# Cross-attention kernel: bias sums in sixteen rows of one bank, other orders in the setup, in slots 0 to 3 and around the folds of N, and two-batch tiles in slot 10

## The reference, cut to what matters

```python
def _L0_xattn_ref(x, latents, shift, scale, ...):    # x: layernormed context, latents: x
    xn = layernorm(x, ln1_w, ln1_b)                   # context, 16 batches x 64 rows x 512
    ln = layernorm(latents, ln2_w, ln2_b)             # 16 batches x 1024 rows x 512
    q = ln @ Wq                                       # 16 heads x 64
    k, v = split(xn @ Wkv, 2)
    q = q * (1.0 + scale[:, None, :, None]) + shift[:, None, :, None]
    attn = softmax(einsum('bihd,bjhd->bhij', q, k) * DIM_HEAD ** -0.5)
    return einsum('bhij,bjhd->bihd', attn, v) @ Wout
x = x + _L0_xattn_ref(ctx_1024, _layernorm(x), fside, fside, ...)
x = x + tanh(((_layernorm(x) @ weight) @ aux_weight1) @ aux_weight2 + ffn_bias)
```

## Time and profile before

| what | value |
|---|---|
| median of 3 runs | 2051.66 us (2050.03 to 2053.55) |
| the profiled execution's own time | 2051.34 us |
| its span in the trace | 2049.5 us |
| PE busy | 2027.4 us (99%) |
| DVE, POOL, ACT busy | 1520.5, 1349.7, 1319.4 us |
| granted TensorE clock, mean | 0.999 |
| DMA | q1 holds nearly all: 429.54 MB, 74.6% of 16 engines' span |

### The profile page before, as it was taken

The page is one execution under the profiler, slowest core; times in us unless marked ns, Lnnn a source line. Parts: engine busy times, 40 slices in busy tenths (PEclk is TensorE's granted clock), DMA queues, the critical chain, the costliest instruction groups (busy, mean ns, idle before and its releaser), DMA issues.

```text
span 2049.5 us, 31380 instructions
## 1 busy us (share of the span) xinstructions
PE 2027.4 (99%) x9180; PEld 1681.4 (82%) x9180; DVE 1520.5 (74%) x2414; ACT 1319.4 (64%) x3005; POOL 1349.7 (66%) x1466
## 2 busy tenths in 40 slices
PE   9999999999999999999999999999999999999998
PEld 7777878888888888888888888888888888888887
DVE  7567777776777777777777777777777777787776
ACT  4455667666766666666666667666666666666654
POOL 3136766766676776767676776767677676767564
PEclk9999999999999999999999999999999999999999
DMA  7657988878787887878788787878767576666653
GB/s 263 197 176 211 271 232 245 251 225 248 222 227 206 219 223 208 226 204 231 195 232 219 208 224 206 230 197 217 211 185 211 174 207 179 200 184 191 178 170 118
DMA packets 502490, 431.54 MB, mean 211 GB/s; under 512 B 54832, under 2 KB 408240, under 8 KB 502320
## 3 DMA queue, kind: packets, MB, share of 16 engines
q1 hardware_dynamic: 502320, 429.54, 74.6%
HBM read 251.33 MB, written 178.06 MB: 210 GB/s over the span
## 4 chain that ended last, share of the span: by engine, by line
PE 86%; DVE 3%; DMA 2%; ACT 2%; issue 2%; POOL 2%; SPq 2%; DVEq 0%; ACTq 0%; POOLq 0%
PE bank L161 34%; PE bank L1176 21%; PE bank L166 17%; PE bank L1179 10%; DMA m_scratch<-evac 1%; PE bank L880 1%; PE bank L879 1%; POOL area L1458 1%; POOL area L1465 1%; DVE N_lo L987 0%; DVE area L1319 0%; SPq L321 0%; DVE row_max L1324 0%; DVE turned L1341 0%; ACT bank L992 0%
## 5 line engine op out<-in xcount | busy, mean ns | idle before, releaser
L1458 POOL TENSOR_TENSOR area<-area,row_max 128x256 f32<-128x256 f32 x512 | 353.8, 712 | 145.8 <-DVE row_max L1324 145.8
L1176 PE MATMUL bank<-N_hi,pT_hi 128*128 128x512 f32 x1024 | 398.7, 389 | 2.6 <-DVE N_lo L987 1.3
L161 PE MATMUL bank<-M_hi,xT_hi 128*128 128x512 f32 x1024 | 398.7, 389 | 0.0
L161 PE MATMUL bank<-M_lo,xT_hi 128*128 128x512 f32 x1024 | 398.7, 389 | 0.0
L1176 PE MATMUL bank<-N_lo,pT_hi 128*128 128x512 f32 x1024 | 398.6, 389 | 0.0
L1227 ACT CAST pT_hi<-turned 128x512 fp32r<-128x512 f32 x256 | 159.1, 622 | 337.4 <-DVE turned L1341 337.4
L1465 POOL TENSOR_TENSOR area<-area,row_inv 128x512 f32<-128x512 f32 x256 | 269.2, 1052 | 114.7 <-DVE row_inv L1333 114.6
L1482 POOL TENSOR_TENSOR area<-area 128x512 f32<-128x512 f32 x127 | 165.4, 1303 | 239.3 <-ACT area L1266 239.3
L1330 DVE TENSOR_REDUCE row_sum<-area 128x8 f32<-128x512 f32 x256 | 174.4, 681 | 167.5 <-ACT area L1222 166.7
L1350 DVE TENSOR_TENSOR pT_lo<-turned,pT_hi 128x512 fp32r<-128x512 f32 x256 | 196.1, 766 | 119.2 <-ACT pT_hi L1227 119.2
L166 PE MATMUL bank<-M_hi,xT_lo 128*128 128x512 f32 x1024 | 273.9, 389 | 0.8 <-POOL xT_lo L1025 0.7
(11 more groups left out here) (183 smaller groups left out, 3923.3 us busy)
## 6 DMA issues: line engine op xcount, KB each, us to landing
p_scratch<-area SPq DMA_DIRECT2D x256, 256.0 KB, 2.6
p_moved<-p_scratch SPq DMA_DIRECT2D x512, 128.0 KB, 4.3
area<-x_dram SPq DMA_DIRECT2D x128, 256.0 KB, 4.5
area<-x_turned_dram SPq DMA_DIRECT2D x128, 256.0 KB, 4.0
x_scratch<-area SPq DMA_DIRECT2D x127, 256.0 KB, 3.0
x_moved<-x_scratch SPq DMA_DIRECT2D x508, 64.0 KB, 3.5
y_dram<-area SPq DMA_DIRECT2D x127, 256.0 KB, 3.6
land<-m_scratch SPq DMA_DIRECT2D x120, 256.0 KB, 2.8
```

Source lines behind the costliest of these rows:

```text
L161: mm = eng.matmul(ps, sh, mv, start=(n == 0), stop=False)
L1176: pe.matmul(O_ps[:], st(pT_hi, k), n_cols(mv, k), start=(k == 0 and mv is N_hi), stop=False)
L1458: last = pool.tensor_tensor(s, s, row.to_broadcast([P, 2, 4, J2]), ALU.subtract)
```

## The change

- **Bias sums.** The ones become one column a head in the block `bdv`; with a shifted window of it (`to_row`) the stationary operand has its ones in one row position a head, so that the eight pairs of a half, two matmuls each, accumulate in sixteen rows of one bank, one bank a half. PE no longer waits for an evacuation between them; ACT evacuates twice 16 rows instead of 16 times 128. The stores are still 32 DMAs: sixteen of half 0 beside kv 28 to 31, sixteen of half 1 in slots 0 to 3, four a slot, after place C's store. The load of x tile 6, in slot 4, waits for all of them, since it takes their buffer.
- **Setup orders.** Separate lists for SP, ACT, DVE and POOL after the front. PE does turn 3 before w3_lo 3 and turns 4 to 7 one kv later; ACT does turns 4 to 7 after the evacuations of kv 3, 5, 6 and 7; DVE goes on with its context tiles without standing between kv steps; POOL takes the low parts of chunks 11 and 13 too. The load of context tile 7 stands after kv 3 and behind a chunk load that waits for chunk 10's split.
- **M1 stores.** m1_raw takes its pieces in another order; slot 0 waits for the first four stores only. Slot 0 waits for the bias evacuations 1 and 2 (before: 15 and 16).
- **Slots 0 to 3.** xT_hi of tile 0 is made by POOL instead of ACT; POOL subtracts the maximum of half 0 before xT_lo of tile 1 in slot 0, and makes xT_lo(t+1) before it normalises in slots 2 and 3.
- **Folds of N.** ACT and DVE do folds 0 and 1 first, then the P work, with ACT's folds 2 to 7 after pT_hi, and DVE's fold 2 between `turn_p` and pT_lo, folds 3 to 7 after.
- **Tiles.** Tiles 28 to 31 stand in slot 10 instead of 9, all later ones a slot later. Tile 28 waits for the low part of fold 6; slot 9's fold 2 waits for the sum of tile 26 (`s_tsum` 27).

```diff
 pe_steps: ("w3_hi", 3), ("w3_lo", 3), ("turn", 3)  ->  ("w3_hi", 3), ("turn", 3), ("w3_lo", 3)
+        W3_LO = (2, 3, 0, 1)
-            some("turn", 2, 3) + some("split", 7, 8) + some("w3", 0, 1, 2, 3) + [("stats", 4), ("norm", 4)]
+            some("turn", 2, 3) + some("split", 7, 8) + some("w3", *W3_LO[:2]) + [("stats", 4), ("norm", 4)] + some("w3", *W3_LO[2:]) + \
+            [("stats", 5), ("norm", 5), ("turn", 4), ("split", 10), ("stats", 6), ("norm", 6), ("turn", 5), ("stats", 7), ("norm", 7)] + \
+            some("turn", 6) + some("split", 12) + some("turn", 7)
+        beside_sp = {2: some("split", 10), 3: some("load", 7), 4: some("split", 11), 6: some("split", 12), 8: some("split", 13),
+                     24: [("k0_load", 0)], 27: [("x0", 0)]}
+        beside_act = {0: some("split", 10), 1: some("split", 11), 3: some("turn", 4), 4: some("split", 12), 5: some("turn", 5),
+                      6: some("turn", 6), 7: some("turn", 7) + some("split", 13), 26: [("k0", 0)], 27: [("k0", 1)]}
-            pe_steps += [("kv", n)] + ([("turn", {1: 4, 3: 5, 4: 6, 5: 7}[n])] if n in (1, 3, 4, 5) else [])
+            pe_steps += [("kv", n)] + ([("turn", {2: 4, 4: 5, 5: 6, 6: 7}[n])] if n in (2, 4, 5, 6) else [])
-        POOL_LO = (6, 9)
+        POOL_LO = (6, 9, 11, 13)
...
         def load_x(sp, u, r):
             at_least(sp, s_xout[r], 16 * (u // RING))
+            if u == 6:
+                sp.wait_ge(s_kbst[1], 16 * H)
+        def store_bias(sp, half, four):
+            q, h = four // 2, four % 2
+            if four == 0:
+                sp.wait_ge(s_kbo, half + 1)
+            rows = bias_scratch[half * 8:half * 8 + 8].rearrange("b (q h s k j) -> q h k b s j", q=2, h=2, s=2, k=4)[q, h]
+            own = bias_out[half][four * 4:four * 4 + 4, :].rearrange("k (b s j) -> k b s j", b=8, s=2)
+            for k in range(4):
+                sp.dma_start(rows[k:k + 1], own[k:k + 1]).then_inc(s_kbst[half], 16)
...
-                tile_at[2 + m, place] = 4 * m + i
+                tile_at[2 + m + m // (TPB - 1), place] = 4 * m + i
...
             store("C")
+            if t < 4:
+                store_bias(sp, 1, t)
...
                     if t == TPB + 1 and p == 2:
-                        pe.wait_ge(s_tsum, 31)
+                        pe.wait_ge(s_tsum, 27)
... slot_act
+            folds = m == 1 and 1 < t < T
+            if folds:
+                fold_n_act(act, t - 1, range(2))
             if tile_of(t - 1):
                 pT_hi_part(0, t - 1)
             if m == 0 and 0 < t < T:
                 v_prepare_act(act, t // TPB)
-            if m == 1 and 1 < t < T:
-                fold_n_act(act, t - 1, range(8))
+            if folds:
+                fold_n_act(act, t - 1, range(2, 8))
... slot_dve
+            if folds:
+                fold_n_dve(dve, t - 1, range(2))
...              turn_p(0, t - 1)
+                if folds:
+                    fold_n_dve(dve, t - 1, range(2, 3))
                 pT_lo_part(0, t - 1)
-            if m == 1 and 1 < t < T:
-                fold_n_dve(dve, t - 1, range(8))
+            if folds:
+                fold_n_dve(dve, t - 1, range(3, 8))
... slot_pool
+            if t in (2, 3):
+                xT_split_lo(pool, t + 1)
             if t < T:
                 normalise(0)
                 normalise(1)
```

More of the change, by code:

```diff
@@ L173, in build @@
         RING_W = 5
-        m1_raw = [stage_more[:, i * BANK:(i + 1) * BANK] for i in range(4)] + xr[2:4] + [S[0][:, i * BANK:(i + 1) * BANK] for i in range(2)]
+        M1_EARLY = 4
+        m1_raw = [S[0][:, i * BANK:(i + 1) * BANK] for i in range(2)] + xr[2:4] + [stage_more[:, i * BANK:(i + 1) * BANK] for i in range(4)]
         stage = stage + [stage_more[:, i * 2 * D:(i + 1) * 2 * D] for i in range(2)]
@@ L211, in build @@
[L211 to L216, removed]
@@ new lines, in build @@
+        beside_dve = {27: [("k0", 0)], 28: [("k0", 1)]}
+        for g in range(4):
+            beside_dve[(9, 10, 12, 14)[g]] = some("fold", g)
+            beside_act[11 + 2 * g] = some("split", WQ_FIRST + g)
+            beside_dve[11 + 2 * g] = some("split", WQ_FIRST + g)
+            beside_sp[11 + 2 * g] = some("split", WQ_FIRST + g)
+            beside_act[(20, 22, 25, 28)[g]] = some("split", WQ_FIRST + 4 + g)
+            beside_dve[(21, 23, 26, 29)[g]] = some("split", WQ_FIRST + 4 + g)
@@ L226, in build @@
             pe_steps += [("kb", n - 19)] if 19 <= n < 31 else []
-            later_steps += [("kv", n)] + beside.get(n, [])
+            sp_later += [("kv", n)] + beside_sp.get(n, [])
+            act_later += [("kv", n)] + beside_act.get(n, [])
+            dve_later += [("kv", n)] + beside_dve.get(n, [])
+        pool_later = [("kv", n) for n in range(4 * PAIRS)]
         kv_where = lambda n: (1 - n // 16, (n // 8) % 2, n % 8)
@@ L251, in build @@
         s_ku, s_kuh, s_kul, s_kb, s_kbo = (sem(n) for n in ("s_ku", "s_kuh", "s_kul", "s_kb", "s_kbo"))
-        s_kbst = [sem(f"s_kbst{i}") for i in range(3)]
+        s_kbst = [sem(f"s_kbst{i}") for i in range(2)]
         s_kvst = [sem(f"s_kvst{i}") for i in range(2)]
@@ L279, in load_ctx @@
                 sp.dma_start(ctx_in[i % 3], ctx_t[i]).then_inc(s_ctx[i % 3], 16)
[L281 to L287, removed]
             for c in range(5):
@@ L362, in setup_pool @@
             pool.wait_ge(s_const, 3)
-            for step, i in pool_front + later_steps:
+            for step, i in pool_front + pool_later:
                 if step == "stats":
@@ L392, in setup_act @@
         def setup_act(act):
-            for step, i in act_front + later_steps:
+            for step, i in act_front + act_later:
                 if step == "split":
@@ L442, in setup_dve @@
             for half in range(2):
-                own = slice(half * DH, (half + 1) * DH)
-                dve.memset(bdv[own, own].bitcast(F32), 1.0).then_inc(s_ones, 1)
-            for step, i in dve_front + later_steps:
+                dve.memset(bdv[half * DH:(half + 1) * DH, ONE_AT[half]:ONE_AT[half] + 1].bitcast(F32), 1.0).then_inc(s_ones, 1)
+            for step, i in dve_front + dve_later:
                 if step == "stats":
@@ L532, in bias_sums @@
             pe.wait_ge(s_kul, k + 1)
-            at_least(pe, s_kbo, k - 1)
-            pe.matmul(kb_ps[k % 2][:], head_ones, ku_hi[k % 2][:], start=True, stop=False)
-            pe.matmul(kb_ps[k % 2][:], head_ones, ku_lo[k % 2][:], start=False, stop=True).then_inc(s_kb, 1)
+            half, p = k // PAIRS, k % PAIRS
+            row = p // 4 * 8 + p % 4
+            to_row = bdv[:, ONE_AT[0] - row:ONE_AT[0] - row + P]
+            pe.matmul(kb_ps[half][:], to_row, ku_hi[k % 2][:], start=(p == 0), stop=False)
+            pe.matmul(kb_ps[half][:], to_row, ku_lo[k % 2][:], start=False, stop=(p == PAIRS - 1)).then_inc(s_kb, 1)
         def setup_pe(pe):
@@ L682, in load_bias @@
             if b < 2:
-                for i, w in enumerate(s_kbst):
-                    sp.wait_ge(w, 32 * len(range(i, PAIRS if b == 0 else 2 * PAIRS, 3)))
+                sp.wait_ge(s_kbst[b], 16 * H)
             sp.dma_start(bias, bias_scratch[bass.ds(b, 1), :].to_broadcast([P, INNER])).then_inc(s_bin, 16)
```

97 lines of the change are left out of this document (48 added, 49 removed).

## The result

The changed kernel takes 2082.65 us (median of 5 runs, 2080.05 to 2082.72), the kernel before 2051.66 us (median of 5 runs as well): a ratio of 1.0149, with a 95% interval of 1.0135 to 1.0162. It is slower by 31.0 us; 25.8 were forecast. 2082.65 lies in the range of 2066 to 2083, near its upper end and 0.65 us above the 2073 to 2082 given for the main case.

What follows compares the result with a forecast made beforehand. PE, busy 99% of the span, was taken to bound the kernel. From 2051.34 us the terms 25.85 - 2.2 - 2.65 + 1.3 - 1.4 + 4.9 gave +25.8, 2077.1 us, with a range from 2066 to 2083.

Steps and rivals of the forecast that it cites:

- main case: Whole kernel: all terms of the sum as forecast, about 2077 us (2073 to 2082), chance 0.45.
- Folds: Fold slots: folds 6 and 7 wait for low parts of N, 2.0 us a slot; thirteen slots +26.0, slot 25 +1.15.
- cascade: Fold slots: low parts 4 and 5 later than the next scores, or folded P late at O; 2091 us, chance 0.08.
- Slot 9: Fold slot 9: three earlier waits, 3.3 us with restarts, of which 2.0 come back; -1.3 us.
- Bias sums and the fold of M: Setup: kb's waits for ACT's evacuation go, -2.2 us; PE's wait for banks at the fold of M goes, -2.65.
- Setup orders: Setup: a turn's 1.5 us wait goes, but context tile 7 lands later and kv 8 begins at 61.2, not 59.89; +1.3 us.
- Slots 0 to 3: Slots 0 to 3: first O waits some 0.5 us less, tile 4's wait for xT_lo goes (0.9); -1.4 us.
- SP's queue: Slots 3 to 6: half 1's bias stores delay k_raw loads; PE stalls about 1.0, 3.4 and 0.5 us; +4.9 us.
- What was there to win: PE's waits: few and single, nearly all in the setup and slots 0 to 9; about 10 us in 2050.
- hidden lag: Rival, slots 4 to 6: fold cost as forecast, but SP's lag costs 0; 2072.2 us, chance 0.30.
- faster case: Rival, fold slots: fold 6 isn't late and folds cost 0; 2042 us, 2047 with SP's lag; chance 0.07.
- cheaper folds: Rival, fold slots: 1.5 us a slot; 2066 us with SP's lag hidden, 2070.5 with it; chance 0.08.

Runs made afterwards that it cites:

- Experiment 1: The changed kernel with ACT's and DVE's order in the fold slots as in the kernel before; 2056.51 us, 1.0032.
- 2: The kernel before with only the new order of ACT and DVE in the fold slots; 2078.65 us, 1.0142.
- Experiment 3: The changed kernel with ACT's cast of fold 2 moved ahead of pT_hi, DVE as changed; 2066.36 us, 1.0082.
- 11: Experiment 9 with DVE's folds 0 to 4 ahead of the turn and ACT's folds 0 to 5 ahead of pT_hi; 2043.58 us, 0.9965.
- 12: The changed kernel with DVE's folds 0 to 4 ahead of the turn and ACT's folds 0 to 5 ahead of pT_hi; 2053.09 us, 1.001.
- experiment 5: Experiment 4 with the low parts of chunks 11 and 13 made by DVE instead of POOL; 2052.69 us, 1.0009.
- experiment 4: Experiment 1 with half 1's bias stores moved out of slots 2 and 3 into slots 0 and 1; 2049.58 us, 1.0001.
- experiment 9: Experiment 6 with two DMAs instead of four for four bias rows, half 1's all in slot 0 ahead of P's store; 2046.94 us, 0.9985.
- 6: Experiment 4 with the setup orders of the kernel before, but the sixteen-row bias sums; 2052.34 us, 1.0011.
- Experiment 7: Experiment 6 with the loads of x and of x transposed of slots 2 to 7 issued by ACT instead of SP; 2054.5 us, 1.0021.

## Why the prediction was right, and where not

- **Folds.** Right in mechanism, place and size: 27.5 us in 14 slots, 27.15 forecast. Fold 6 at 5.45, fold 7 at 6.65, 2.0 a slot; measured 5.46, 6.67 and 2.01. Experiments 1 and 2 show it from both sides. Experiment 3 shows that half of it is ACT's place ahead of fold 2; the other half, DVE's ahead of fold 3, is read from the timelines and wasn't moved by itself, but 11 and 12, which move both, lose nothing. No cascade came.
- **Slot 9.** Forecast -1.3, measured +0.5 with slot 10. The waits of tile C and of the tile's sum went, as said. What the sum lacked is the clock: behind the 1.46 and 0.23 us waits of slot 9 comes a stretch at the lower level that costs 1.7 us (below).
- **Bias sums and the fold of M.** Right: between 80 and 160 us PE loses 0.2 us instead of 5.4, a gain of 5.2, 4.85 forecast.
- **Setup orders.** Mis-sized: +1.3 forecast, +3.7 measured up to 80 us (from the same ledger, 12.3 against 8.6, of which 0.9 falls in the first 25 us). The wait at kv 8 is there, 1.9 us (2 forecast), but kv 8 starts at 63.49 instead of 61.2, since turn 7 stands at 58.23 instead of 56.0. Turns 6 and 7 wait 2.15 and 1.5 us. Turn 6's wait comes from a DVE instruction stretched beside POOL's new low part, and experiment 5 shows that it only hides turn 7's. The working began tile 7's norm at the landing, put at 52.9; it landed at 53.89, and DVE began at 55.07. In its order stands the low part of turn 5 ahead of it. That waited for ACT, and ACT, one step earlier in its order, for the store of an earlier product to free its buffer, a wait that the working had at nothing. ACT, then DVE:

```profile
53.35 0.59 ACT L431 COPY area<-bank 128x512 f32<-128x512 f32 x1 [3.76 <-DMA kv_scratch<-area]
```

```profile
54.46 0.69 DVE L484 TENSOR_TENSOR N_lo<-bank,N_hi 128x512 fp32r<-128x512 f32 x1 [1.26 <-ACT N_hi L427]
55.07 0.69 DVE L451 BATCH_NORM_STATS2 area<-area 128x6 f32<-128x512 f32 x1
```

- **Slots 0 to 3.** Half right: tile 4's wait for xT_lo went (0.9 of the 1.4), but the first O waits as long as before (1.4 against 1.3 us), so the 0.5 didn't come.
- **SP's queue.** Slots 0 to 8 lose 4.5 more, 3.5 forecast with the -1.4. The forecast lag is there: the second load of k_raw in slot 3 issues at 194.71 instead of 192.89, 1.8 later. But that is less than the 2.1 to spare, so the lag alone gives no stall in slot 4, and the 1.0 forecast doesn't follow from the numbers beside it. The stall, 1.8 us, came because PE, without its waits further ahead, was at tile A 2.6 us sooner (197.3 without the stall, against 199.90), while the low part of k_parts was ready 1.2 later (199.04 against 197.83). 1.6 us more go to the lower clock behind it. Slot 5's 3.4 didn't come. In slot 6 1.3 us came instead of 0.5, but experiment 4 shows that most of it is no lag of the bias stores. So the sum of this term came near by luck, its parts were not right. What the prediction took from the Trainium skill, DMA: Bandwidth & Descriptors, section "Issuing engines are not separate DMA queues", that the stores would cost next to nothing wherever they stand, doesn't hold in this kernel: moving eight of them took slot 4's wait away, and merging them was worth 5.4 us in experiment 9 against 6.
- **What was there to win.** The prediction's list of PE's waits leaves out four (1.5, 1.5, 1.3 and 0.5 us): they come to 16 us, not some 11. No term of its sum rests on that.
- **Rivals.** The hidden lag is out by slot 4's wait, the faster case and the cheaper folds by the 1.22 and 0.24 us waits of every fold slot.
- **Still open.** Experiment 1 lies 6.6 us above before instead of 2 to 3. Its trace has tile A's waits of 2.4 us and two stretches at the lower clock in the setup, 1.5 us each, but experiment 4's trace has such stretches too. Three of its six executions, at 2057.8 to 2058.0 us, have a mean granted clock of 0.997, the other three, at 2053.9 to 2055.3, 0.998 to 1.000; what they did differently no trace shows. Why experiment 7 lost is open too. Since one execution's first 25 us differ by 1 to 2 us from the next one's, differences below that between single traces aren't read as effects.

## What to carry to other kernels

Where two engines follow a third through a ring of buffers, count for each instruction put between them what the ring has in hand: four banks gave 0.5 us here, and the P work put in around fold 2 cost 2.0 us a slot, the same work put in after fold 4 (DVE) and fold 5 (ACT) nothing. Before moving something to save a wait, look whether the engine that would start sooner waits for the bottleneck anyway, as ACT and DVE did at folds 0 and 1. And a gain in the setup shows only if the queue that carries the next stage's transfers gains too; look at it for transfers that one DMA could do instead of four.

## What the runs showed of the hardware

- **The clock behind a wait.** Behind the 1.80 us wait of PE in slot 4, eight matmuls of 512 columns are 0.43 us apart instead of 0.23, 1.6 us lost; granted clock by window (PE, PEld, DVE, ACT, POOL busy, then PEclk), 0.59 there, which is the level of 1.2 GHz for most of it, and 1.00 again from 204 us:

```profile
199.20:203.40 4.20, 4.20 (x13) 3.33 (x14) 4.13 (x8) 3.06 (x9) 1.43 (x2) 0.59 0.73 219
204.00:208.00 4.00, 4.00 (x21) 3.35 (x20) 2.49 (x7) 3.43 (x10) 2.94 (x4) 1.00 0.85 252
292.00:295.60 3.60, 3.60 (x10) 2.79 (x11) 3.23 (x6) 1.37 (x4) 0.73 (x1) 0.53 0.00 1
```

It doesn't follow every such wait: the kernel before shows none behind its 2.49 us wait, nor the changed one behind 2.15 us at 53.35, while experiment 1 has one behind the same wait, with the same setup orders.
- **DVE beside POOL.** The DVE instruction that started at 50.44 ended at 53.21, 0.56 us after POOL's ended at 52.65, instead of taking 0.75 us. In experiment 5, with no POOL work beside it, it took 0.75. A second one, at 64.08 beside POOL's other new low part (63.73 to 66.29), took 2.76 us instead of 0.69 and ended 0.55 after POOL's:

```profile
64.08 2.76 DVE L494 SCALAR_TENSOR_TENSOR area<-stage_more,area 128x512 f32<-128x512 f32 x1
```

The Trainium skill, SBUF — State Buffer, section "SBUF: two separate sides", says that within the engines only the port pair shared by GpSimd and DVE causes contention; the trace agrees as far as these two go; whether nothing else contends it can't show. In both cases DVE ended some 0.55 us after POOL, less than the 0.69 to 0.75 us that its instruction takes alone, so it did most of its work only then, which fits an engine that stood still rather than one that ran slower.
- **An issue's time.** A store of one row of 2 KB occupied SP for 622 ns, one of half of four rows, 4 KB, for 320 ns (medians).
